# Four attention heads on four TensorE row groups instead of one head at a time, with extra full-size matmuls

## What is computed

```python
h = _layernorm(x, axis=-1) * (1 + ca) + sa
q = (x @ wq).reshape(B, T, H, D)              # B 2, T 1024, H 16, D 8
lat = x @ w_down
k = (lat @ wk_up).reshape(B, T, H, D)
v = (lat @ wv_up).reshape(B, T, H, D)
q = _apply_rope(q, cos, sin)
k = _apply_rope(k, cos, sin)
scores = jnp.einsum('bqhd,bkhd->bhqk', q, k) * scale
pages = jnp.arange(T) // PAGE_SIZE            # 32 tokens to a page
allowed = pages[None, :] <= pages[:, None]
scores = jnp.where(allowed[None, None], scores, jnp.finfo(scores.dtype).min)
attn = jax.nn.softmax(scores, axis=-1)
out = jnp.einsum('bhqk,bkhd->bqhd', attn, v).reshape(B, T, E)
x = x + ga * (out @ wo)
```

## Time and profile before

| | us |
|---|---|
| median of 3 runs | 768.57 |
| lowest, highest | 767.8, 771.25 |
| the profiled execution | 771.94 |
| its span (first to last instruction) | 770.1 |
| PE busy in the span | 681.2 (88%) |
| DVE busy | 588.5 (76%) |
| ACT busy | 520.4 (68%) |
| mean granted clock of PE | 0.94 |

### The profile page before, as it was taken

The page is one execution under the profiler, slowest core; times in us unless marked ns, Lnnn a source line. Parts: engine busy times, 40 slices in busy tenths (PEclk is TensorE's granted clock), DMA queues, the critical chain, the costliest instruction groups (busy, mean ns, idle before and its releaser), DMA issues.

```text
span 770.1 us, 12222 instructions
## 1 busy us (share of the span) xinstructions
PE 681.2 (88%) x3976; PEld 427.2 (55%) x4000; DVE 588.5 (76%) x1133; ACT 520.4 (68%) x905; POOL 183.8 (24%) x144
## 2 busy tenths in 40 slices
PE   3920988999699999987599999999999999999996
PEld 2410222333233333345478777787777877778885
DVE  5670987888588888229678898888988889888775
ACT  2530035677476777973488888888888888888984
POOL 0451016000000000000223343333433344322322
PEclk9965579999899999998799999999999999999998
DMA  9541041100101000000111110011100111101200
GB/s 237 150 139 65 0 117 40 43 21 25 46 2 44 24 20 4 3 1 1 66 45 55 56 56 28 29 56 56 55 34 24 54 56 57 54 2 55 69 15 28
DMA packets 17413, 37.20 MB, mean 48 GB/s; under 512 B 3305, under 2 KB 11241, under 8 KB 14533
## 3 DMA queue, kind: packets, MB, share of 16 engines
q1 hardware_dynamic: 16037, 34.65, 13.9%
q10 hardware_dynamic: 1312, 1.74, 0.9%
HBM read 31.86 MB, written 4.33 MB: 47 GB/s over the span
## 4 chain that ended last, share of the span: by engine, by line
PE 33%; DVE 12%; issue 5%; ACT 1%; POOL 0%; POOLq 0%; DVEq 0%
DVE gel_lo L1049 6%; PE y L952 6%; PE y L954 5%; PE y L953 5%; PE hid L943 5%; PE hid L942 5%; PE hid L941 5%; PE plog L963 2%; DVE part L1105 1%; ACT gel_hi L1017 1%; DVE at_least L1077 1%; PE pcw L972 1%; DVE cw L1096 0%; DVE cw L1094 0%; DVE dl L1084 0%
## 5 line engine op out<-in xcount | busy, mean ns | idle before, releaser
L1049 DVE TENSOR_TENSOR gel_lo<-gel,gel_hi 128x512 fp32r<-128x512 f32 x256 | 248.3, 1010 | 6.7 <-ACT gel_hi L1017 5.7
L588 DVE TENSOR_REDUCE mcol<-mx 128x1 f32<-128x512 f32 (+2 forms) x320 | 193.1, 635 | 61.7 <-PE mx L704 58.8
L562 ACT ACTIVATE probs<-st 128x512 f32<-128x512 f32 x288 | 155.7, 596 | 99.3 <-PE st L660 57.1
L1016 ACT ACTIVATE gel<-hid,b_sb 128x512 f32<-128x512 f32 x256 | 176.1, 688 | 38.5 <-PE hid L943 16.2
L1017 ACT ACTIVATE gel_hi<-hid,b_sb 128x512 fp32r<-128x512 f32 x256 | 174.7, 682 | 0.0
L1157 POOL TENSOR_TENSOR cur<-cur,part 128x512 f32<-128x512 f32 x64 | 106.4, 1663 | 250.8 <-DVE part L1105 250.8
L704 PE MATMUL mx<-ks,qs 125*128 125x512 bf16 (+3 forms) x384 | 120.8, 364 | 38.3 <-PEq L208 32.0
L952 PE MATMUL y<-gel_hi,w_hi 128*128 128x512 f32 x256 | 104.4, 408 | 0.4 <-DVE gel_lo L1049 0.2
L941 PE MATMUL hid<-cur_hi,w_hi 128*128 128x512 f32 x256 | 102.2, 399 | 0.4 <-DVE cur_lo L1123 0.4
L943 PE MATMUL hid<-cur_hi,w_lo 128*128 128x512 f32 x256 | 102.2, 399 | 0.0
L942 PE MATMUL hid<-cur_lo,w_hi 128*128 128x512 f32 x256 | 102.1, 399 | 0.0
(11 more groups left out here) (147 smaller groups left out, 521.9 us busy)
## 6 DMA issues: line engine op xcount, KB each, us to landing
cwb<-gate_rows SPq DMA_DIRECT2D x16, 1024.0 KB, 4.7
ks<-in_k_rows SPq DMA_DIRECT2D x3, 640.0 KB
qs<-in_q_rows SPq DMA_DIRECT2D x3, 616.0 KB
q_pieces<-pieces_q SPq DMA_DIRECT2D x4, 384.0 KB, 4.8
k_pieces<-pieces_k SPq DMA_DIRECT2D x4, 384.0 KB, 6.0
ks<-k_pieces SPq DMA_DIRECT2D x8, 192.0 KB
qs<-q_pieces SPq DMA_DIRECT2D x8, 192.0 KB
x_sb<-in_x SPq DMA_DIRECT2D x4, 256.0 KB, 5.2
```

Of the source, the lines that this page charges most:

```text
L562: nc.scalar.activation(probs[u % SLOTS][:, h, :], st[:, (HG * u + h) % ST_RING, :], ACT.Exp, scale=SCALE).then_inc(exp_done, 1)
L588: nc.vector.tensor_reduce(mcol[a % SLOTS][:, h, slot:slot + step * (len(blocks) - 1) + 1:step], mx[:, at % MX_RING, 0:len(blocks) * keys]. ...
L1016: nc.scalar.activation(gel[n % RING][:, :], hid[n % RING][:, :], ACT.Gelu_apprx_tanh, bias=bias)
L1049: nc.vector.tensor_tensor(gel_lo[n % RING][:, :], gel[n % RING][:, :], gel_hi[n % RING][:, :], ALU.subtract).then_inc(lo_ok, 1)
```

## The change

- q and k are split into two pieces of fp32r (a 4-byte type that PE takes in one pass) in place of three of bf16, and a score has 3 terms in place of 6. A head then needs 32 rows: 24 of terms, 2 for the maximum, 4 for the pages within a block of 128 tokens. Four heads fill the 128 partitions of `ks` and `qs`, and head h works on rows 32h to 32h+31, a row group of the array.
- The pieces are written to DRAM in that layout (24 DMAs of 256 KB in place of 8 of 384 KB), and a group is loaded with two DMAs of 128 rows of 4 KB. `second_piece` on ACT and the third piece on POOL are gone.
- A bin is filled for two heads at a time, into two banks, and read by DVE in one instruction of up to 1024 elements: 20 bins for a group in place of 40. The ring is 2 of such pairs. Where a block of 128 keys meets its own queries, the page rows are needed, and that part is a matmul of its own with 30 rows.
- A group has 10 units in place of 9, each of one half of the queries; two of them have 256 columns and ACT does only those. `ov` is one bank in place of two. `weigh` is done once for each unit, not in halves.
- `keep_busy`: ahead of the loop each of the 28 bins is preceded by two matmuls of 512 columns on all 128 rows whose result is overwritten; in the loop one such matmul stands ahead of the first bin of each unit (66 of the 80 units).
- The maxima are split on POOL (2 steps) in place of DVE (5 steps; the merging of the two halves stays on DVE), and go to `qs` by four DMAs in place of one.
- The counted loop is gone: all groups are written out. The load of group 2 is issued at the start of the block.

```diff
-Q_PIECE = [0, 0, 0, 1, 1, 2]
-K_PIECE = [0, 1, 2, 0, 1, 0]
+Q_PIECE = [0, 0, 1]
+K_PIECE = [0, 1, 0]
...
+HROWS = 32
+ROW_MAX = TERMS * D
+ROW_PAGE = ROW_MAX + 2
+ROW_END = ROW_PAGE + 4
...
 UNITS = [
-    [(0, 0, 0, 0, 512)],
-    [(1, 0, 0, 0, 512)],
-    [(0, 2, 0, 256, 256), (1, 6, 256, 256, 256)],
-    [(0, 1, 0, 128, 384), (0, 3, 384, 384, 128)],
-    [(1, 1, 0, 0, 512)],
-    [(1, 2, 0, 0, 512)],
-    [(1, 3, 0, 0, 512)],
-    [(1, 4, 0, 0, 512)],
-    [(1, 5, 0, 128, 384), (1, 7, 384, 384, 128)],
+    (0, [(0, 0, 0, 512)]),
+    (0, [(1, 0, 128, 384), (3, 384, 384, 128)]),
+    (0, [(2, 0, 256, 256)]),
+    (1, [(0, 0, 0, 512)]),
+    (1, [(1, 0, 0, 512)]),
+    (1, [(2, 0, 0, 512)]),
+    (1, [(3, 0, 0, 512)]),
+    (1, [(4, 0, 0, 512)]),
+    (1, [(5, 0, 128, 384), (7, 384, 384, 128)]),
+    (1, [(6, 0, 256, 256)]),
...
+PAIRS = HG // 2
+NBINS = len(BINS) * PAIRS
 LEAD = 4
...
+TURN_AFTER = 2 * PAIRS
+BUSY_FIRST, BUSY_LATER = 2, 1
...
-            m.ks = [ma.sb(f"ks{s}", [P, HG, T], BF16) for s in range(SLOTS)]
-            m.qs = [ma.sb(f"qs{s}", [P, HG, T], BF16) for s in range(SLOTS)]
+            m.ks = [ma.sb(f"ks{s}", [P, T], F32R) for s in range(SLOTS)]
+            m.qs = [ma.sb(f"qs{s}", [P, T], F32R) for s in range(SLOTS)]
...
-    for first, n in LOADS:
-        rows = slice(first * D, (first + n) * D)
-        sp.dma_start(m.ks[s][rows, :, :],
-                     m.kp[0:n, g].rearrange("c (d h) t -> c d (h t)", d=D)).then_inc(m.qk_in[s], 16)
-        one = m.qp[Q_PIECE[first]:Q_PIECE[first] + 1, g].rearrange("c (d h) t -> c d (h t)", d=D)
-        sp.dma_start(m.qs[s][rows, :, :], one.broadcast_to([n, D, HG * T])).then_inc(m.qk_in[s], 16)
+    for dst, src in ((m.ks[s], m.kp), (m.qs[s], m.qp)):
+        sp.dma_start(dst[:, :].bitcast(F32), src[g].rearrange("h r t -> (h r) t")).then_inc(m.qk_in[s], 16)
...
-                    sp.dma_start(dst.rearrange("c g r t -> (g r) c t")[b * P:(b + 1) * P, :, at],
-                                 pieces[side][:, c, :, :]).then_inc(pieces_out, 16)
+                    for term, x in enumerate(which):
+                        sp.dma_start(rows[:, D * term:D * (term + 1), at],
+                                     pieces[side][:, c, x, :].bitcast(F32)).then_inc(pieces_out, 16)
...
-    ST_RING, MX_RING = 3, 3
+    ST_RING, PROBS, MX_RING = 3, 3, 2
...
-    ov = l.ps("ov", [P, 2, CH])
-    mx = l.ps("mx", [P, MX_RING, CH])
+    ov = l.ps("ov", [P, CH])
+    mx = l.ps("mx", [P, MX_RING, PAIRS, CH])
...
+                for h in range(HG):
+                    n = 2 * JB
+                    sp.dma_start(m.qs[s][HROWS * h + ROW_MAX:HROWS * h + ROW_MAX + 2, :].bitcast(F32),
+                                 mrow[n * h:n * (h + 1), :]).then_inc(mrow_in[s], 16)
...
+                nc.gpsimd.tensor_copy(hi.bitcast(F32R), nm).then_inc(mchain, 1)
+                pool.wait_ge(mchain, CHAIN * g + 2)
+                nc.gpsimd.tensor_tensor(lo.bitcast(F32R), nm, hi, ALU.subtract).then_inc(mchain, 1)
...
+                nc.scalar.activation(probs[k % PROBS][:, h, 0:n], st[:, (HG * k + h) % ST_RING, 0:n], ACT.Exp,
+                                     scale=SCALE).then_inc(exp_done, 1)
...
-            def scores(i, a, u, h):
-                s, n = a % SLOTS, HG * (NU * gnum(i, a) + u) + h
+            def scores(k, h):
...
-                pe.wait_ge(exp_done, n + 1 - ST_RING + EXP_CREDIT)
-                for c, j, off, q0, nq in UNITS[u]:
-                    mm = nc.tensor.matmul(st[:, (HG * u + h) % ST_RING, off:off + nq],
-                                          m.ks[s][:, h, j * P:(j + 1) * P],
-                                          m.qs[s][:, h, c * CH + q0:c * CH + q0 + nq], start=True, stop=True)
+                    pe.wait_ge(m.qk_in[s], 32 * uses(g))
+                    pe.wait_ge(mrow_in[s], 16 * HG * uses(g))
+                if n >= ST_RING:
+                    pe.wait_ge(exp_done, n + 1 - ST_RING)
+                for j, off, q0, nq in blocks:
+                    own = P if j // TPC == c else 0
+                    for rows, x, w in ((ROW_END, 0, own), (ROW_PAGE, own, nq - own)):
+                        if w:
+                            mm = nc.tensor.matmul(st[:, n % ST_RING, off + x:off + x + w],
+                                                  m.ks[s][r0:r0 + rows, j * P:(j + 1) * P],
+                                                  m.qs[s][r0:r0 + rows, c * CH + q0 + x:c * CH + q0 + x + w],
+                                                  start=True, stop=True)
                 mm.then_inc(st_done, 1)
...
+            def weigh(k):
...
+                pe.wait_ge(exp_done, HG * (k + 1))
+                if u == 0:
+                    pe.wait_ge(vs_ok, g + 1)
+                if u in FIRST_UNIT and 2 * g + c > 0:
+                    pe.wait_ge(ov_read, 2 * g + c)
+                for j, off, q0, nq in blocks:
                     for h in range(HG):
-                        mm = nc.tensor.matmul(ov[32 * h:32 * h + 32, c, q0 + lo - off:q0 + hi - off],
-                                              vs[s][:, j, h, :], probs[u % SLOTS][:, h, lo:hi],
-                                              start=(u == FIRST_UNIT[c] and half == 0),
-                                              stop=(u == LAST_UNIT[c] and half == 1),
+                        mm = nc.tensor.matmul(ov[32 * h:32 * h + 32, q0:q0 + nq],
+                                              vs[s][:, j, h, :], probs[k % PROBS][:, h, off:off + nq],
+                                              start=u in FIRST_UNIT, stop=u in LAST_UNIT,
                                               skip_group_check=True)
-                if half == 1:
-                    mm.then_inc(pv_done, 1)
...
+            def fill_bin(g, n):
+                s, at = g % SLOTS, bin_at(g, n)
+                b, pair = divmod(n, PAIRS)
+                if n == 0:
+                    pe.wait_ge(m.qk_in[s], 32 * uses(g))
+                if at >= MX_RING:
+                    pe.wait_ge(bin_read, at + 1 - MX_RING)
+                keep_busy(g, n)
                 blocks, keys, _, _ = BINS[b]
                 for x, (t, k0) in enumerate(blocks):
-                    mm = nc.tensor.matmul(mx[:, at % MX_RING, x * keys:(x + 1) * keys],
-                                          m.qs[s][0:ROW_MAX, h, t * P:(t + 1) * P],
-                                          m.ks[s][0:ROW_MAX, h, k0:k0 + keys], start=True, stop=True)
+                    own = P if k0 + keys == (t + 1) * P else 0
+                    for rows, y, w in ((ROW_MAX, 0, keys - own), (ROW_END, keys - own, own)):
+                        for i in range(PAIRS):
+                            r0 = HROWS * (2 * pair + i)
+                            if w:
+                                mm = nc.tensor.matmul(mx[:, at % MX_RING, i, x * keys + y:x * keys + y + w],
+                                                      m.qs[s][r0:r0 + rows, t * P:(t + 1) * P],
+                                                      m.ks[s][r0:r0 + rows, k0 + y:k0 + y + w], start=True, stop=True)
...
+            def keep_busy(g, n):
+
+                at = bin_at(g, n)
+                for i in range(BUSY_FIRST if NBINS * g + n < PAIRS * (NU + LEAD) else BUSY_LATER * (n % PAIRS == 0)):
+                    nc.tensor.matmul(mx[:, at % MX_RING, i, :], m.ks[g % SLOTS][:, 0:P], m.ks[g % SLOTS][:, 0:CH],
+                                     start=True, stop=True)
...
+            for unit in range(NU + LEAD):
+                for pair in range(PAIRS):
+                    bins(unit, pair)
+            for k in range(STEPS):
+                scores(k, 0)
+                scores(k, 1)
+                bins(k + NU + LEAD, 0)
+                scores(k, 2)
+                if k >= 1:
+                    weigh(k - 1)
+                bins(k + NU + LEAD, 1)
+                scores(k, 3)
+            weigh(STEPS - 1)
```

More of the change, by code:

```diff
@@ L189, in prep @@
     ro = [l.sb(f"ro{s}", [P, 2, CH]) for s in "qk"]
-    rr = [l.sb(f"rr{s}", [P, CH]) for s in "qk"]
-    pieces = [l.sb(f"pieces_{s}", [P, NCH, 3, CH], BF16) for s in "qk"]
+    pieces = [l.sb(f"pieces_{s}", [P, NCH, 2, CH], F32R) for s in "qk"]
     turned = [l.ps(f"turned{i}", [P, CH]) for i in range(2)]
@@ L724, in body @@
-            def body(i, a):
-                for u in range(NU):
-                    nxt, side = following(i, a, u), part_at(i, a, u)
-                    for half in range(2):
-                        if exists(*nxt[:2]):
-                            scores(*nxt, 2 * half)
-                            scores(*nxt, 2 * half + 1)
-                        if exists(*side[:2]):
-                            part(*side, 2 * half)
-                        weigh(i, a, u, half)
-                        if exists(*side[:2]):
-                            part(*side, 2 * half + 1)
-                    if side[2] == 0 and exists(i, a + 1) and not exists(*side[:2]):
-                        turn_maxima(i, a + 1)
@@ new lines, in bins @@
```

(12 more changed lines are left out.)

379 lines of the change are left out of this document (132 added, 247 removed).

## The result

The changed kernel takes 901.16 us (median of 4 runs, 900.69 to 903.16), the kernel before 769.05 us on the same chip (767.8 to 771.25). The ratio is 1.172, with a 95% interval of 1.169 to 1.175. The forecast was 726 us, range 707 to 800: wrong in size and in sign.

The account below looks back on a forecast made before the run. It took PE to bound the old loop and the ring of three `st` banks the new. Attention ends at 61 + 30 + 174 + 32 = 297 instead of 339.3 us, giving 729.6 profiled and 726 us by median; range 707 to 800.

Parts of the forecast that it names:

- The start at 61: End of prep: with wide loads and stores attention starts at 61 us (bounds 56 and 73) instead of 75.4.
- Row groups overlap: Scores and bins: matmuls on different row groups run at once, as the weigh's column groups do; three scores take 0.25 us.
- rival 2: Scores and bins: row groups don't overlap, so PE needs 3.25 us a unit, 34.3 a group; 777 us; chance 0.14.
- the ring's round: Loop: three `st` banks bound a unit, from third score through weigh and exponential back to PE: 2.64 us, 1.77 with 256 columns.
- rival 1: Bins ahead of the loop and loop: PE's clock stays at half, 41 us a group, 847 us; chance 0.15.
- The prediction's own sign of being wrong: Loop and prep: DVE's wait for PE beyond 20% of the loop, or loads ending prep later than 70 us.
- break-even: Loop: the half clock decides from 32.8 us a group on, which is 3.3 a unit.
- changes of row groups: Loop: if each cost all of a matmul's tail, 0.14 us more a round, 9 us in sum; not adopted.
- the group: Loop: eight units of 512 columns and two of 256 make 24.6 us, 26.4 with added waits, against 29.2 before.
- added waits: Each group: the weigh waits twice for ACT's copy of `ov`, 0.4 us each; row maxima are late by some 1.0 us.
- Rival 4: Loop: stays at 29.2 us a group as DVE, ACT and PE wait in turn; 745 us; chance 0.57 together with the forecast.
- The last units: The last 14 units, without bins: 31 us of rounds and 1 for `ov`, 32 us in all.

Follow-up runs that it names:

- e9: The kernel before with its bins and scores contracting 32 rows in place of 125 and 128: 929.09 us, ratio 1.204.
- e6: The changed kernel with 20 full matmuls ahead of the first and of the last pair of bins before the loop, two extras a unit: median 842.15 us.
- e17: The changed kernel with 74 full matmuls in PE's idle time and 3 extras a unit, but 2, 1 or 0 in four units of single groups: 842.26 us.
- e11: The changed kernel with 64 full matmuls in PE's idle time, 33 extras a group, units without bins filled from the third on: median 794.79 us.
- e16: The changed kernel with 74 full matmuls in PE's idle time, 23 extras a group, all units without bins filled: median 783.97 us, ratio 1.012.
- e10: The kernel before with its bins and scores contracting 64 rows in place of 125 and 128: 928.8 us, ratio 1.203.
- e1: The changed kernel with 20 more full matmuls on 128 rows ahead of the first pair of bins: 891.33 us, ratio 1.156.
- e3: The changed kernel without its own extra matmuls, but with 20 full matmuls ahead of the first pair of bins: 878.31 us, ratio 1.138.
- e4: The changed kernel with 20 more matmuls ahead of the first pair of bins, on 32 rows only: 910.6 us, ratio 1.181.
- e13: The kernel before with the load of group 1 issued at the start of attention in place of inside prep: 760.14 us, ratio 0.986.

## Why the prediction was wrong, point by point

- **The start at 61**: right. PE's first extra matmul stands at 61.05, its first bin at 62.17; the loads and stores of 43 to 61 us ran at 298 GB/s. The timeline of SP (issues of three stores each):

```profile
44.78 3.42 SPq L218 DMA_DIRECT2D q_rows<-pieces_q  x3
53.13 1.86 SPq L218 DMA_DIRECT2D k_rows<-pieces_k  x3
```

- **Row groups overlap**: right (a pair of bins lasts as long as one matmul, 0.58 us), so rival 2 is out. What the changes of mode cost is not settled: see the ring's round below.
- **The step that failed is the clock**, which the prediction had as rival 1 with 0.15 and left outside its range. The observation for it was the right one (a full matmul each 0.60 us at 0.50 ahead of the loop). The argument against it was wrong: "in the loop and the last units PE ran at 1.00 with gaps of 1 us, and at half clock the new loop would leave PE no gap at all" takes PE's busy share for what holds the clock. The changed kernel's PE is busy for 295.5 of 296.8 us at 0.50, and e9 has PE busy without a gap at 0.50. What I should have compared is how much of the array each kernel's matmuls use: 125 and 128 rows before, 24 to 30 after (the weighs are alike in both). Rows alone do not decide either: ahead of the loop the kernel before has 125 rows, PE busy for 28.82 of 31.60 us, and 0.50. The prediction's own sign of being wrong showed as well: DVE sat idle for 146 of the loop's 296.8 us, 49% and not under 20%.
- **Rival 1's price** was too low: 847 us by its sum, 901 measured. Ahead of the loop 54 us, not 40; a group 45.2, not 41; the last 14 units 56, not 46. Its break-even, 3.3 us a unit, was passed by a wide margin: a unit took 4.5.
- **The ring's round**: 2.64 us forecast for a unit of 512 columns. At clock 1.00 with two extras (e6), the second, fourth, fifth, sixth and seventh unit of a group take 2.57, 3.00, 2.53, 2.95 and 2.84 us, 2.78 in the mean: nearly right, and an extra or two are hidden in it (e17). The 0.14 us above the sum are as much as the prediction gave to changes of row groups, but two of the five rounds lie below 2.64, and no run takes these changes out, so their cost stays open. But **the group** was mis-sized: 26.4 us forecast, 29.2 measured at 1.00 with 2 extras. The two units with only 256 columns take 2.51 us each instead of 1.77, so halving the columns saved almost nothing there (1.5 us in all). The eighth and ninth unit, beside which the narrow bins stand (up to eight matmuls of 128 columns in a pair), take 3.55 and 3.57 instead of 2.64 (1.8 us). The first takes 3.19 (0.6), the other five 0.7 more in all. Of these 4.6 us the sum had 1.8 as added waits; 2.8 were missing. Rival 4 (the loop keeps 29.2 us a group) thus had the right number for a loop at full clock, with one extra more; its reason, three engines that wait for each other in turn, was not tested.
- **The last units**: 32 us forecast; at 1.00, with three extras in most or all of them, 38.6 in e11 and 40.1 in e16 (from the first exponential of the first of these units to the last weigh).
- **A reading**: "the last of 12 that begin at 332.72" is the first of the 12; they end at 339.16. The 0.08 us from ACT back to PE is not changed by it.
- Even with the clock held the forecast's 726 us would have been missed: 770 us by the estimate above, with the extras that hold it, not 726.

What stays open is why the clock, once raised, stays up for long in one run and falls in the next of the same kernel (814.5 and 907.1 us), and where in between 64 and 125 rows the kernel before tips: 64 were too few.

## What to carry to other kernels

Before splitting the array into row groups, ask what the clock will be, for a row group uses a quarter of the rows per matmul. A matmul on few rows can keep PE busy all the time at half clock, and then four heads at once are slower than one at a time at full clock (45 against 29 us a group here). Test it first with the cheapest run there is: the old kernel with fewer rows. And take a gain apart before paying for it: 12.3 of the 14.4 us gained at the start were to be had by moving one group's loads, without the new layout.

## What the runs showed of the hardware

- The granted clock of PE depends on how many rows the matmuls use. Loop of the kernel before, same instructions: 125 and 128 rows 1.00, 64 or 32 rows 0.50, with PE busy for 51.3 of 51.3 us (e9, e10). Burst of 20: 128 rows raised it (e1, e3), 32 rows didn't (e4).
- Idle time lowers it as well: 1.00 ahead of a wait of 5.28 us in the kernel before, 0.50 behind it.
- Matmuls on different row groups run at the same time: two of 256 columns and 24 rows last 0.58 us as a pair, and one of them 0.576.
- The clock can rest at either level under the same work: with 2 extras a unit (e6) 108.6 to 166.5 us at 1.00, then 105.7 us at 0.50, then 1.00 again.
- Extra full matmuls can pay for themselves: medians of 901.9 us with one a unit and 817.5 with three (best runs 814.5 and 806.1), and 784.0 with the idle time filled too (e16).
- Narrow loads ahead of stores in SP's queue hold up the stores: with one group's six loads (8 to 24 rows each) moved behind them, the last store is issued by 55.3 us in place of 67.6 (e13).
